# The up-projections' normalized rows: turned through DRAM and VectorE in place of TensorE

## The reference, cut to what matters

```python
# x: (4, 512, 1024); up_w: (1024, 2048), fc1_w: (1024, 512), gate_w: (1024, 8)
x = x + attention(_layernorm(x), ctx)            # "x1" in the kernel
z = _layernorm(x)                                # over the 1024 columns
h = relu(z @ up_w) ** 2
x_latent = z @ fc1_w
routing = top_k(z @ gate_w, 2)
...
x = x + _layernorm(h @ down_w + routed, gamma, beta)
```

## Time and profile before

| | us |
|---|---|
| median of 3 runs | 2131.2 (2129.99 to 2131.87) |
| the profiled execution's own time | 2130.59 |
| its span | 2128.8 |
| TensorE busy in it | 2105.7 |
| ScalarE busy | 695.0 |
| VectorE busy | 790.7 |
| GpSimd busy | 754.3 |

### The profile page before, as it was taken

The page is one execution under the profiler, slowest core; times in us unless marked ns, Lnnn a source line. Parts: engine busy times, 40 slices in busy tenths (PEclk is TensorE's granted clock), DMA queues, the critical chain, the costliest instruction groups (busy, mean ns, idle before and its releaser), DMA issues.

```text
span 2128.8 us, 30459 instructions
## 1 busy us (share of the span) xinstructions
PE 2105.7 (99%) x9724; PEld 1738.9 (82%) x9724; DVE 790.7 (37%) x1401; ACT 695.0 (33%) x1206; POOL 754.3 (35%) x616
## 2 busy tenths in 40 slices
PE   8999999999999999999999999999999999999998
PEld 7888888877888888878888878787878888888886
DVE  4231311277888878831101313121321232222233
ACT  5111211167777777741111223111123311111111
POOL 3533030156777777662212343010114422222221
PEclk9999999999999999999999999999999999999999
DMA  6743432635655555444334343222223632222222
GB/s 198 265 148 138 172 118 95 181 83 130 165 147 142 151 150 134 128 115 149 127 120 158 127 165 129 104 80 82 79 69 134 203 101 89 87 80 87 78 85 71
DMA packets 231518, 269.51 MB, mean 127 GB/s; under 512 B 77457, under 2 KB 145297, under 8 KB 230545
## 3 DMA queue, kind: packets, MB, share of 16 engines
q1 hardware_dynamic: 186592, 196.58, 29.9%
q10 hardware_dynamic: 44848, 71.97, 11.0%
HBM read 175.93 MB, written 92.29 MB: 126 GB/s over the span
## 4 chain that ended last, share of the span: by engine, by line
PE 97%; DVE 1%; issue 1%; ACT 0%; DMA 0%; POOL 0%; ACTq 0%; SPq 0%; DVEq 0%; POOLq 0%
PE psum L117 30%; PE psum L118 30%; PE psum L119 30%; PE psum L980 3%; PE psum L231 1%; PE psum L1034 1%; PE psum L1035 1%; PE psum L1017 1%; PE psum L1016 1%; PE psum L1650 0%; PE psum L1649 0%; PE psum L989 0%; DMA staging<-in_wqkv 0%; DVE small L180 0%; DMA staging<-in_ctx 0%
## 5 line engine op out<-in xcount | busy, mean ns | idle before, releaser
L117 PE MATMUL psum<-operands 128*128 128x512 f32 (+3 forms) x2888 | 1116.9, 387 | 10.9 <-DVE operands L352 9.6
L118 PE MATMUL psum<-operands 128*128 128x512 f32 (+3 forms) x2888 | 1110.6, 385 | 0.0
L119 PE MATMUL psum<-operands 128*128 128x512 f32 (+3 forms) x2888 | 1108.4, 384 | 0.0
L117 PEld LDWEIGHTS psum<-operands 128*128 128x128 f32 (+1 forms) x2888 | 543.6, 188 | 111.4 <-DVE operands L352 9.4
L119 PEld LDWEIGHTS psum<-operands 128*128 128x128 f32 (+1 forms) x2888 | 544.1, 188 | 107.3
L118 PEld LDWEIGHTS psum<-operands 128*128 128x128 f32 (+1 forms) x2888 | 544.6, 189 | 93.4
L1276 POOL TENSOR_TENSOR operands<-staging,operands 128x512 fp32r<-128x512 f32 x92 | 118.3, 1296 | 368.3 <-ACT operands L1271 367.5
L1162 DVE TENSOR_REDUCE small<-psum 128x1 f32<-128x576 f32 x256 | 192.3, 751 | 96.0 <-PE psum L980 95.9
L1877 POOL TENSOR_TENSOR operands<-operands 128x640 fp32r<-128x640 f32 x64 | 100.8, 1581 | 318.9 <-ACT operands L1872 318.5
L901 POOL TENSOR_TENSOR operands<-staging,operands 128x512 fp32r<-128x512 f32 x128 | 164.4, 1292 | 36.8 <-ACT operands L1084 28.0
L1729 DVE TENSOR_TENSOR staging<-staging 128x512 f32<-128x512 f32 x64 | 45.3, 726 | 305.4 <-ACT staging L1695 304.6
(11 more groups left out here) (112 smaller groups left out, 1318.3 us busy)
## 6 DMA issues: line engine op xcount, KB each, us to landing
h_scratch<-staging ACTq DMA_DIRECT2D x80, 256.0 KB, 2.1
operands<-h_scratch SPq DMA_DIRECT2D x64, 320.0 KB, 3.1
operands<-recip_scratch SPq DMA_DIRECT2D x64, 192.0 KB, 3.9
o_scratch<-staging SPq DMA_DIRECT2D x64, 192.0 KB, 4.5
operands<-o_scratch SPq DMA_DIRECT2D x64, 192.0 KB, 2.6
operands<-q_hi_scratch ACTq DMA_DIRECT2D x14, 768.0 KB, 5.9
operands<-q_lo_scratch ACTq DMA_DIRECT2D x14, 768.0 KB, 5.9
staging<-in_x SPq DMA_DIRECT2D x20, 512.0 KB, 3.9
```

The source lines that it names most:

```text
L117: e.matmul(o, lh, rh, start=first, stop=False)
L118: e.matmul(o, lh, rl, start=False, stop=False)
L119: return e.matmul(o, ll, rh, start=False, stop=last)
```

## The change

z of batches 1 to 3 isn't turned on TensorE any more (z of batch 0 still is). Instead ACT stores the normalized rows to a DRAM tensor `z_d` (one DMA of 2 MB, behind group 2's stores), and loads them back in 32 DMAs of 64 KB, sixteen behind group 3's stores and sixteen behind group 4's. Each puts 32x32 blocks in place: 32 partitions, 16 blocks along the free dimension, with 32 elements (128 bytes) in a run, 512 runs to a DMA. VectorE turns the 32x32 blocks of one chunk in one instruction of 128x512 into PSUM bank 6 or 7 (`d_turn`). The load of x1 moves ahead of group 0's jobs, the normalization and its square root move from group 2 to group 1, and in each group that has z DMAs they stand ahead of the group's jobs. `XB` is the same memory as `XN2`.

```diff
+    z_d = dram("z_scratch", (S, D))
...
+        XB = SF[:, D:D + ST * D].rearrange("p (k s) -> p k s", k=DK)
+        d_zs, d_bl = sem("d_z_stored"), [sem(f"d_blocks_loaded{h}") for h in range(2)]
+
+        def d_z_out(e, b):
+
+            e.wait_ge(*past(d_zn, b + 1))
+            e.dma_start(z_d.rearrange("(t p) d -> p t d", p=P), XN2).then_inc(d_zs, 16)
+
+        def d_blocks_in(e, b, h):
+
+            if h == 0:
+                e.wait_ge(*past(d_zs, b * 16))
+            for k in range(4 * h, 4 * h + 4):
+                for g in range(P // 32):
+                    e.dma_start(XB[32 * g:32 * g + 32, k, :].rearrange("p (u j) -> p u j", j=32),
+                                z_d.rearrange("(u i) (k g j) -> k g i u j", i=32, g=4, j=32)[k, g]).then_inc(d_bl[h], 16)
+
+        def d_turn(e, b, k):
+
+            if k % 4 == 0:
+                e.wait_ge(*past(d_bl[k // 4], b * (4 * 64)))
+            e.wait_ge(*past(d_zl, b * DK + k - 1))
+            e.transpose(PS[:, 6 + k % 2, :], XB[:, k, :]).then_inc(d_zt, 1)
...
@@ d_pe
-            def pet(e, b, k):
-                if k == 0:
-                    e.wait_ge(*past(d_gc, b * GC))
-                d_pet0(e, b, k)
...
-                mm_groups(e, b, D_GROUPS, d_zl, wait_bank, job_slot, d_acc, slot_ready, gate, d_fr, None if last else pet)
+                mm_groups(e, b, D_GROUPS, d_zl, wait_bank, job_slot, d_acc, slot_ready, gate, d_fr)
...
@@ d_act
-                    run(g, b)
                     if g == 0 and not last:
                         d_load(e, x1_d, b + 1)
                     if g == 2 and not last:
+                        d_z_out(e, b + 1)
+                    if g in (3, 4) and not last:
+                        d_blocks_in(e, b + 1, g - 3)
+                    run(g, b)
+                    if g == 1 and not last:
                         d_sqrt(e, b + 1)
...
@@ d_dve
                     final = g == len(D_GROUPS) - 1 and not last
+                    for k in range(2 if final else 0):
+                        d_turn(e, b + 1, k)
                     for k in range(DK - 1 if final else 0):
                         d_lo(e, b + 1, k)
+                        if k + 2 < DK:
+                            d_turn(e, b + 1, k + 2)
...
-                    if g == 2 and not last:
+                    if g == 1 and not last:
                         d_norm(e, b + 1)
```

More of the change, by code:

```diff
@@ L244, in dve_lo @@
                 e.tensor_tensor(zlo[:, k, :], z_bank(b, k), raw(zhi[:, k, :]), ALU.subtract).then_inc(zl, 1)
-            return load, load_tile, dve_norm, act_center, act_scale, act_sqrt, pe_t, act_hi, dve_lo, zl, fr, zt, zh, ch, cp
+            return load, load_tile, dve_norm, act_center, act_scale, act_sqrt, pe_t, act_hi, dve_lo, zl, fr, zt, zh, ch, cp, zn
         def mm_groups(e, b, groups, lo_sem, wait_bank, slot_of, done, slot_ready=None, after_group=None, free=None, pe_t=None, bank=None):
@@ L483, in xattn_ffn_kernel @@
         A_EV = NQK + ST
-        a_load, a_load_tile, a_norm, a_center, a_scale_z, a_sqrt, a_pet, a_hi, a_lo, a_zl, a_fr, a_zt, a_zh, a_ch, a_cp = norm_z(
+        a_load, a_load_tile, a_norm, a_center, a_scale_z, a_sqrt, a_pet, a_hi, a_lo, a_zl, a_fr, a_zt, a_zh, a_ch, a_cp, _ = norm_z(
             "a", XN, lambda e, b: e.wait_ge(*past(a_acc, b * A_EV)), (5, 6, 7), True)
@@ L1325, in xattn_ffn_kernel @@
         d_acc = sem("d_product", 20)
-        d_load, _, d_norm, _, _, d_sqrt, d_pet0, d_hi, d_lo, d_zl, d_fr, d_zt, _, _, _ = norm_z(
+        d_load, _, d_norm, _, _, d_sqrt, d_pet0, d_hi, d_lo, d_zl, d_fr, d_zt, _, _, _, d_zn = norm_z(
             "d", XN2, lambda e, b: e.wait_ge(*past(d_acc, b * ND)))
+        XB = SF[:, D:D + ST * D].rearrange("p (k s) -> p k s", k=DK)
[15 more added lines that the diff above has]
+            e.transpose(PS[:, 6 + k % 2, :], XB[:, k, :]).then_inc(d_zt, 1)
         NQ = 4
```

## The result

| | us |
|---|---|
| median before, 5 runs | 2130.59 (2129.99 to 2131.87) |
| median after, 5 runs | 2141.21 (2140.0 to 2144.44) |
| ratio | 1.0051, 95% [1.0039, 1.0062] |
| the profiled execution after, and its span | 2141.08, 2139.1 |
| TensorE busy in it | 2099.3 |

What follows compares the result with a forecast made beforehand. TensorE was taken as the bound, with 97% of the chain. Batch 1 starts 12.0 us late through ACT; less 2 x 3.8 saved, +4.4; with 1.5 for the clock, +5.9: median 2137.1 us, range 2126 to 2151.

Steps and rivals of the forecast that it cites:

- The saving: Stage d, batches 1 to 3: 32 transposes taken off TensorE save 3.8 us each, 11.4 us in all.
- group 3's stores over: Batch 0, ACT: the stores end at 1305, or 1302.6 if the 2 MB cost nothing, 1306.5 if late.
- first sixteen issues, I: Batch 0, behind group 3's stores: sixteen DMA issues hold ACT 0.55 us each, 8.8 us (5.4 to 9.8).
- batch 1's start: Batch 1's first matmul comes at 1349.6 against 1337.59 before, 12.0 us late, from ACT's path in batch 0.
- The two waits' lengths: TensorE in batch 0 waits about 10.7 us before the last group and about 5 before batch 1's first matmul.
- The normalization's place: Batch 0, ACT: the moved normalization holds up group 2's second and third store by about 4.5 us.
- rival 1: Issues hardly hold ACT; all 11.4 us are kept, 2119.8 us; chance 0.17.
- the turnings: VectorE: eight turnings of 128x512 at 0.65 to 0.69 us each, hidden in batches 1 and 2 by the last group.
- the packets: DMA queues: a half's 8192 packets take 7.8 to 17.9 us, 10 taken; at 10 hidden in batch 0.
- rival 3: Packets or turning are slow as well: 2155 to 2175 us, or 2143 with the slow turning alone; chance 0.12.
- The clock: TensorE runs at a lower clock after its waits; the second wait costs up to 2.8 us, 1.5 taken.
- Rival 2: Same mechanism, issues of 0.35 to 0.45 us, no clock loss: within 0.2%, about 2131 us; chance 0.23.

Runs made afterwards that it cites:

- Experiment 6: Changed kernel with batch 0 entirely as before the change; only z of batches 2 and 3 goes through DRAM and VectorE: 2124.51 us, ratio 0.9953 to the kernel before.
- experiment 10: Repeat in more rounds of the changed kernel with batch 0 entirely as before the change: 2122.82 us, ratio 0.9964 to the kernel before.
- experiment 9: Kernel before plus only the earlier load of x1 and earlier normalization with its square root; TensorE still turns z: 2133.06 us, ratio 1.0013.
- experiment 3: Changed kernel without the 32 block loads per batch; z still stored, VectorE turns the rows as they lie: 2127.73 us, ratio 0.9973 to the kernel before.
- experiment 2: Changed kernel with all 32 block loads issued by SP, behind group 3's weight loads, instead of ACT: 2131.6 us, ratio 0.9995 to the kernel before.
- experiment 7: Changed kernel with each block load cut in two, 64 DMAs of 256 runs, same bytes: 2181.85 us, ratio 1.0231 to the kernel before.

## Why the prediction was right, step by step

**The direction and the mechanism** came out as put: two runs of sixteen issues in batch 0, a wait ahead of the last group, a second ahead of batch 1, none in batches 1 and 2. Experiment 6 takes both away, and what is left is the saving alone. The size came out only roughly, and is inside the stated range in part because that is 25 us wide: 10.6 us for 5.9. Of the 4.7 that are missing, 2.9 lie in stage d, and its terms follow; 1.8 lie outside the stage, nearly all of it in the later start that I put down to scatter.

**The saving.** 3.8 us for each batch: experiments 6 and 10 give 7.6 and 7.7 for two.

**The path in batch 0,** in the prediction's terms. The starts after are taken less 1.6, by which batch 0's gate came later:

| term | forecast | measured |
|---|---|---|
| group 3's stores over | 1305 | 1307.89 - 1.6 = 1306.3 |
| first sixteen issues, I | 8.8 | 1318.54 - 1307.89 = 10.65 |
| group 3's jobs | 12.75 | 1330.28 - 1318.54 = 11.74 |
| group 4's evacuation and stores | 3.0 | 1333.26 - 1330.28 = 2.98 |
| second sixteen issues | 8.8 | 1342.64 - 1333.26 = 9.38 |
| to the first `zhi` | 2.7 | 1345.24 - 1342.64 = 2.60 |
| to batch 1's first matmul | 8.5 | 1353.85 - 1345.24 = 8.61 |
| batch 1's start | 1349.6 (+12.0) | 1352.25 (+14.7) |

14.7 - 7.6 + 1.65 (below) makes +8.7, and the stage's length grew by 8.8. The mis-sized terms are "sixteen take I = 8.8 us", off by 1.85 and 0.6, and "stores over at 1305", off by 1.3; the jobs gave 1.0 back. The second has an error of its own working: from group 3's evacuation to the end of its stores it left 2.1 us (1302.9 to 1305), where the sum has 3.0 for the same step of group 4; that is 0.9 of the 1.3. I took the issue at 0.55. In batch 1 it was 8.66/16 = 0.54, as taken; in batch 0 the mean was 0.67 and 0.59. Taken one by one, most of batch 0's issues start 0.54 apart too. The excess lies in a few early ones: in the first run, three of the first five take 1.29, 1.40 and 0.94; in the second none takes more than 0.85. The changed kernel's second profile has 1.16, 1.44 and 0.94 at the same places (10.46 and 8.86 for sixteen), so it isn't scatter; its cause stays open.

**The two waits' lengths.** The first, 10.92 against 10.7, agrees in part by chance: the last group's start, less 1.6, was 2.2 us later than forecast, and TensorE was itself 1.8 us later there, by the wait ahead of group 4. The second came out at 2.94 instead of about 5: the last group's matmuls ran slowly behind the first wait and took 18.8 us instead of 16.3 (starts 1331.96 to 1350.53, and one step of 0.227).

**The normalization's place** was in the sum only through ACT ("hold up group 2's second and third store by about 4.5 us"): group 2's jobs were to start at 1287.6 and started at 1290.19 - 1.6 = 1288.6. That the same delay makes TensorE wait ahead of group 4 was not seen, and the prediction had no term for it. It came out right in spite of this: in the changed kernel this wait (1.48 us) costs nothing more, since ACT, not TensorE, sets when the last group and batch 1 begin. Where it stands alone it is worth 3.9 us in the profile (experiment 9). It is why experiment 3, and in part why experiment 2, came out above what I expected. Had the issues been free, rival 1's 2119.8 would have been missed by some 5 us: experiment 3, which has no block loads, shows 6.3 of the 11.4.

**Hidden by other work, as said:** the turnings and the packets. The turning takes 0.727 us at the median (0.65 to 0.69 taken), and `zhi` after `zhi` starts 1.34 apart (1347.36, 1348.70 above), where 1.3 was taken. A block DMA lands in 2.2 us at the median and 4.0 at most, so no backlog built up. The price of a packet came out a little below the lower of the two that were taken. ACT's queue in the window 1311.5:1318.5 of the changed kernel, with hardly anything but the 128 byte runs in it (packets, MB, share of 16 engines):

```profile
q10 hardware_dynamic: 6365, 0.81, 72.9%
```

0.729 x 16 x 7 / 6365 = 12.8 ns, so a half's 8192 packets take about 6.6 us of the 16 engines (an estimate), where 7.8 to 17.9 were the ends and 10 was taken. That is less than the 8.7 to 10.7 us in which a half is issued, so the issues hide it; at rival 3's 35 ns they would not have.

The Trainium skill's "VectorE: DVE Perf Modes" (The three transpose paths) warns of strided DMA copies for turning, if the inner step is large. Here the turning proper stays on VectorE and the DMA keeps runs of 32 elements; its landings of 2.2 us don't show such a slowdown, and no run here makes the copy that the page warns of.

**The clock.** Forecast 1.5 for the second wait. The rows at 1353.85 and after: matmuls of 0.63 us. Eight of them, up to the one at 1357.31, take 3.46 us where eight at 0.227 take 1.8: 1.65 lost. The windows after:

```profile
1331.00:1340.00 9.00, 8.04 (x25) 6.42 (x26) 1.48 (x2) 0.83 (x2) 0.71 (x1) 0.67 0.87 211
...
1354.00:1360.00 6.00, 6.00 (x20) 4.79 (x21) 2.38 (x5) 2.42 (x5) 2.54 (x2) 0.72 0.43 160
```

The granted clock is 0.67 and 0.72 behind the two waits, between its levels of 1.2 and 2.4 GHz; behind the first one it costs time that is hidden behind ACT's issues.

**Rivals.** Rival 1 (issues hardly hold ACT) falls with the rows at 1307.89 and 1333.26, and with experiment 7. The Trainium skill's "DMA: Bandwidth & Descriptors" (Anatomy of one DMA) gives the sequencer's part as about 50 ns, but for a DMA that GpSimd issues. So it was no measure for ACT's queue, as the prediction had it: by that figure sixteen issues would take an estimated 0.8 us, and these runs show 8.2 to 10.65. Rival 2, which needed issues of 0.35 to 0.45 us, fell with 0.54. What stays open is what an issue's half microsecond consists of, and why a few of batch 0's early ones take up to 1.4 us; and the changed kernel with only its normalization put back wasn't run.

## What to carry to other kernels

A DMA issue is work of the engine that issues it, here about half a microsecond for a strided load of 64 KB and nearly as much for one of 32 KB. It shows not as busy time but as idle time, often with the releaser "issue" and at times with that of an engine long done. Count the issues that a change puts into an engine's order, find the batch in which that order has least slack, and price the change there: the same 32 block loads cost 15 us in batch 0 and nothing in batches 1 and 2. A step that is moved earlier takes its waits with it, so look at what stands behind it in its new place. And if one iteration of a loop has no room for a change, peel it off: the saving of the others was to be had whole.

## What the hardware did that I had not expected

- The time of an issue goes by the DMA. From start to start it is 0.54 us with 512 runs and 0.50 with 256, with two of over 1 us near the start of batch 0's first run in every kernel with the block loads on ACT's queue; on SP's queue 18.01 / 32 = 0.56 on average.
- The packets of 128 bytes took about 13 ns of a DMA engine each.
- Loads of 64 KB in runs of 128 bytes landed in 2.2 us, and in 2.0 with half the runs.
- After a wait of 1.48 us TensorE's matmuls took 0.50 and then 0.40 us, and the granted clock of the window 1293:1299 was 1.00. After one of 2.09 us (experiment 9) the first four took 0.39 to 0.51, the seven from 1294.17 to 1296.73 took 0.63, and from 1297.50 on they took 0.39 again.
